# Slot 2's product, GpSimd's slot 1 and the third experts' product in another order, and the tail's input and output on two engines

## The reference

```python
x = x + conv(_gn(x), ...)                   # group norm, a graph convolution, residual
t = _to_tokens(x)
t = t + attn(_ln_t(t), ...)                 # a scan over 1024 tokens, 128 channels x 16 states
t = t + ffn(_ln_t(t), ...)                  # 8 experts, the two best of each token
x = _from_tokens(t, x)

def scan_step(h, inputs):                   # inside attn
    x_t, dt_t, B_t, C_t = inputs
    h_new = exp(dt_t[..., None] * A) * h + (dt_t[..., None] * B_t[:, None, :]) * x_t[..., None]
    return h_new, (h_new * C_t[:, None, :]).sum(axis=-1)

probs = softmax(xt @ Wr + br)               # inside ffn
top_p, top_idx = top_k(probs, 2)
weights = top_p / top_p.sum(axis=-1, keepdims=True)
out = (weights[:, :, None] * take(experts(layernorm(xt)), top_idx)).sum(axis=1)
```

## Time and profile before

| | us |
|---|---|
| median of 3 runs | 381.32 |
| runs | 381.15 to 382.72 |
| profiled execution, its own time | 379.5 |
| its span, first to last instruction | 377.8 |
| VectorE busy | 316.5 (84%) |
| TensorE busy | 317.3 (84%) |
| ScalarE busy | 277.9 (74%) |
| GpSimd busy | 268.0 (71%) |

### The profile page before, as it was taken

The page is one execution under the profiler, slowest core; times in us unless marked ns, Lnnn a source line. Parts: engine busy times, 40 slices in busy tenths (PEclk is TensorE's granted clock), DMA queues, the critical chain, the costliest instruction groups (busy, mean ns, idle before and its releaser), DMA issues. The chain is left out here.

```text
span 377.8 us, 5525 instructions
## 1 busy us (share of the span) xinstructions
PE 317.3 (84%) x1675; PEld 176.7 (47%) x1675; DVE 316.5 (84%) x424; ACT 277.9 (74%) x465; POOL 268.0 (71%) x268
## 2 busy tenths in 40 slices
PE   0597899695899889988998899989987997798795
PEld 0476455441555355525553455345534543453563
DVE  2784457998799989998999899989999998999533
ACT  1002458586989998989899989998988894872483
POOL 8903505685688978897799779977998787877110
PEclk9996999577899999999999999999998999999999
DMA  7934039979989989996996699769957985000000
GB/s 182 250 88 86 2 106 220 228 170 218 222 205 225 225 203 208 220 221 161 219 231 159 152 220 219 152 173 217 222 128 193 224 197 125 3 0 1 16 0 16
DMA packets 21301, 59.54 MB, mean 158 GB/s; under 512 B 4988, under 2 KB 13336, under 8 KB 15384
## 3 DMA queue, kind: packets, MB, share of 16 engines
q1 hardware_dynamic: 20104, 58.35, 68.1%
q10 hardware_dynamic: 1168, 0.84, 0.9%
HBM read 53.94 MB, written 5.24 MB: 157 GB/s over the span
## 5 line engine op out<-in xcount | busy, mean ns | idle before, releaser
L356 POOL TENSOR_TENSOR hs<-hs,Cs 128x1024 f32<-128x1024 f32 x63 | 149.3, 2376 | 22.5 <-DVE hs L836 21.8
L836 DVE TENSOR_TENSOR_SCAN hs<-av,P 128x1024 f32<-128x1024 f32 x64 | 146.3, 2286 | 2.6 <-POOL av L349 0.4
L830 DVE TENSOR_TENSOR P<-P,ub 128x1024 f32<-128x1024 f32 x62 | 76.0, 1226 | 3.1 <-DMA ub<-u_scratch 1.9
L676 ACT ACTIVATE hb<-P,b1c 128x512 f32<-128x512 f32 x112 | 70.1, 685 | 2.4 <-PE P L1309 1.0
L1321 PE MATMUL P<-hb,W2s 128*64 128x256 f32 x448 | 60.3, 392 | 0.0
L1308 PE MATMUL P<-X,W1H 128*128 128x512 f32 x112 | 49.6, 443 | 4.3 <-ACT hb L676 3.3
L617 ACT ACTIVATE av<-P,Aneg 128x510 f32<-128x510 f32 x68 | 44.1, 680 | 9.3 <-PE P L1241 5.2
L1309 PE MATMUL P<-X,W1L 128*128 128x512 f32 x112 | 44.5, 398 | 0.0
L1321 PEld LDWEIGHTS P<-hb,W2s 128*64 128x64 f32 x448 | 27.4, 136 | 27.8 <-issue 17.3
L617 ACT ACTIVATE av<-av,Aneg 128x510 f32<-128x510 f32 x60 | 38.3, 708 | 2.6 <-DMA av<-dt_scratch 2.5
L1241 PE MATMUL P<-D,selD 128*128 128x512 f32 x64 | 29.9, 509 | 11.7 <-ACT av L617 11.4
(11 more groups left out here) (230 smaller groups left out, 546.3 us busy)
## 6 DMA issues: line engine op xcount, KB each, us to landing
ub<-u_scratch SPq DMA_DIRECT2D x31, 1024.0 KB, 11.5
av<-dt_scratch SPq DMA_DIRECT2D x15, 1024.0 KB, 7.3
dt_scratch<-dts SPq DMA_DIRECT2D x7, 256.0 KB, 2.9
u_scratch<-rl SPq DMA_DIRECT2D x7, 256.0 KB, 2.9
av<-in_L_conv_Wr SPq DMA_DIRECT2D x2, 576.0 KB, 6.9
av<-in_L_conv_Wl SPq DMA_DIRECT2D x2, 576.0 KB, 8.6
res<-in_x SPq DMA_DIRECT2D x4, 256.0 KB, 4.5
hb<-in_L_ffn_W SPq DMA_DIRECT2D x2, 512.0 KB, 5.9
```

The source lines that it names most:

```text
L356: gp.tensor_tensor(hs[:, at, :, :], hs[:, at, :, :], rep(Cs[:, p, :], 1, 2), ALU.mult).then_inc(S["cm"], 1)
L676: a_.activation(hb[:, r % HB, :], P[:, F1_BANK[r], :], ACT.Gelu, bias=b1c[:, r:r + 1]).then_inc(S["gl"], 1)
L830: v.tensor_tensor(ring, rep(P[:, BB, :], 1, 2), ub[:, 2 * n:2 * n + 2, :], ALU.mult).then_inc(S["bm"], 1)
L836: v.tensor_tensor_scan(hs[:, (SLOTS * g + n) % RING].rearrange("p a t -> p (a t)"), av[:, 2 * n:2 * n + 2, :].rearrange("p a t -> p (a t)" ...
```

## The change

Four things are written in another order or on another engine; nothing that is computed changes.

- On VectorE the function of a slot is cut into its product and its scan. The product of slot 2 stands ahead of the marks, its scan behind them. The product of slot 7 stands ahead of experts(4), its scan behind.
- On GpSimd slot 1 stands between the split and the weights. It waits for the split's own signal first.
- In the tail VectorE scales xn first, then one half of X2; GpSimd copies the other half from xn. The two differences wait for both.
- The second piece of the last group's result is sent by ScalarE's queue instead of SP's.

```diff
-            sp_out(sp_, G - 1, 1)
+            sp_out(sp_, G - 1, 1, (0,))
...
                     pool_x2(eng, prev)
-                    pool_router(eng, prev)
+                    eng.wait_ge(S["xl2"], prev + 1)
                 if i > 0:
                     pool_slot(eng, i, p, 1)
+                if prev is not None:
+                    pool_router(eng, prev)
...
+            eng.wait_ge(S["xn2"], 2 * G)
+            eng.wait_ge(S["f1"], LAST)
+            gp.tensor_copy(X2[0:64, 0:HW], xn[0:64, :]).then_inc(S["xh2"], 1)
             pool_router(eng, G - 1)
...
+            sp_out(eng, G - 1, 1, (1,))
...
                     dve_router1(eng, prev)
+                dve_product(eng, i, 2)
+                if prev is not None:
                     dve_router2(eng, prev, nxt2)
-                dve_slot(eng, i, 2)
+                dve_scan(eng, i, 2)
...
                 dve_slot(eng, i, 6)
+                dve_product(eng, i, 7)
                 experts(4)
-                dve_slot(eng, i, 7)
+                dve_scan(eng, i, 7)
...
-            for h in range(2):
-                q = slice(64 * h, 64 * h + 64)
-                v.tensor_tensor(X2[q, HW * h:HW * h + HW], P[q, XB, 0:HW], rqs[q, :], ALU.mult).then_inc(S["xh2"], 1)
             v.tensor_tensor(xn, P[:, XB, 0:HW], rqs[:, :], ALU.mult).then_inc(S["xn2"], 2)
+            v.tensor_tensor(X2[64:128, HW:T], P[64:128, XB, 0:HW], rqs[64:128, :], ALU.mult).then_inc(S["xh2"], 1)
             eng.wait_ge(S["xn2"], 2 * G)
-            eng.wait_ge(S["xh2"], 2 * G)
-            for h in range(2):
+            for h in (1, 0):
                 q, o = slice(64 * h, 64 * h + 64), slice(64 - 64 * h, 128 - 64 * h)
+                eng.wait_ge(S["xh2"], 2 * G)
```

More of the change, by code:

```diff
@@ L274, in sp_spread, with sp_out @@
                 sp_.dma_start(ub[:, 4 * c:4 * c + 4, :], rep(u_dram[p][:, 4 * c:4 * c + 4, :], 0, ST)).then_inc(S[f"u_in{c}"], 16)
-        def sp_out(sp_, g, p):
+        def sp_out(sp_, g, p, halves=(0, 1)):
             sp_.wait_ge(S["acc"], EXP * (g + 1))
-            for h in range(2):
+            for h in halves:
                 sp_.dma_start(ov[h, :, g:g + 1, :], acc[64 * h:64 * h + 64, 0:1, :]).then_inc(S["out_sem"], 16)
@@ L817, in dve_slot, with dve_product @@
         def dve_slot(eng, g, n):
+            dve_product(eng, g, n)
+            dve_scan(eng, g, n)
+        def dve_product(eng, g, n):
             c = n // 2
@@ L830, in dve_slot, with dve_scan @@
                 v.tensor_tensor(ring, rep(P[:, BB, :], 1, 2), ub[:, 2 * n:2 * n + 2, :], ALU.mult).then_inc(S["bm"], 1)
+        def dve_scan(eng, g, n):
+            c = n // 2
             eng.wait_ge(S["bm"], SLOTS * g + n + 1)
```

## The result

The changed kernel takes **388.41 us** (median; 386.27 to 391.04) against 382.02 (381.15 to 385.41): a ratio of 1.0168, 95% interval 1.0121 to 1.0214. It is slower, as forecast, but by 6.4 us and not by 3.4, and lies above the range. Its profiled execution took 386.95 us with a span of 385.2, against 379.5 and 377.8. The changed kernel's four executions differ in their mean granted clock, from 0.947 in the fastest to 0.925 in the slowest.

A forecast was written before the change was run, and what follows sets the result against it. Bound by a circle of GpSimd's long run and VectorE's scans 2 to 5. Steps lose 4.23 us, the end gains 0.38 and 0.45: 3.40 lost, 384.7 us, range 380.5 to 386.8.

The forecast's parts named there:

- L902 is held to the slot's end: VectorE's TENSOR_SCALAR in the marks waits until GpSimd's slot 1 ends; scan 2 comes 0.44 us later per step; chance 0.64.
- Slot's end to scan 2, 0.50 us: On VectorE, scan 2 follows the end of GpSimd's slot 1 by 0.50 us, as the product did in step 6.
- The sum of the steps, 4.23 us: Loss over steps 1 to 7: 2.20 us in steps 1 to 5, 0.92 in step 6, 1.11 in step 7.
- Third experts' product behind slot 7's, nothing: On VectorE, slot 7's product ahead of the third experts' product saves waits off the circle; costed at nothing.
- the first rival: L902 isn't held by GpSimd's slot: a step shrinks by about 0.42 us, 3.28 in all, 378.0 us; chance 0.16.
- The weights behind the slot: GpSimd's weights end near 217.9, before TensorE transposes them at 218.38, behind expert products that hide the delay.
- The tail's input and output, -0.38 and -0.45 us: In the tail, sharing the input with GpSimd gains 0.38 us; ScalarE issuing the second last transfer gains 0.45.
- the last rival: L902 held, and TensorE's clock falls before the tail: 0.88 us plus some 1.2 more, 386.8 us; chance 0.10.

The follow-up runs named there:

- The run with two halves: Changed kernel with GpSimd's slot 1 cut into two ops of 128x512 each, all orders kept: 381.89 us, ratio 0.9988 to before.

## Why the prediction was right about the steps and wrong about the tail

*L902 is held to the slot's end*: right. 0.08 us from split to slot was 0.08; 1.6 us of hold was 1.9, as L917 asked 0.49 us into the slot and not 0.77; the end, which alone counts, was the slot's end and 0.02 us. The Trainium skill (SBUF — State Buffer, "Who interferes with whom") says the same: who starts first keeps the shared ports for the whole instruction. The run with two halves agrees, with 0.76 us for the instruction, which ends 0.03 behind the first half. The Trainium skill (VectorE: DVE Perf Modes, "Why PSUM operands drop a tier") says that an operand in PSUM keeps an instruction out of the mode that takes both ports; the run with the result in PSUM agrees, 0.15 us beside a slot. Which mode an instruction ran in, no row shows.

*Slot's end to scan 2, 0.50 us*: it was 0.56, nearly the whole difference between the forecast 0.44 us a step and the 0.51 measured.

*The sum of the steps, 4.23 us*: 4.30. Step 6 gave 1.27, of which 0.39 came back ahead of scan 5 (forecast 1.21 and 0.29), step 7 gave 1.14 (forecast 1.11).

*Third experts' product behind slot 7's, nothing*: right by itself (382.30 us), and the steps of this kernel add up with it at nothing, though no run takes it out of this kernel alone. Wrong for the case without the hold, where it lets slot 2's gain through. So the first rival was mispriced. A step without the hold gains 0.62 us instead of the 0.42 I allowed. As I read it, I took TensorE's waits as the limit and did not see that the third experts' product, and not slot 7's scan, is what has to wait for TensorE. The trace of the kernel with PSUM shows 3.63 us gained from scan 1 of step 1 to the last scan and 0.68 behind it, 4.3 us in all against the 3.28 of the rival. The ratio of the times says 5.9 us, while the two profiled executions stand only 3.3 apart, since this one took 1.0 us longer up to scan 1 of step 1. Where the rest lies, no trace shows.

*The weights behind the slot*: hidden as costed; VectorE's list of waits shows none on TensorE's expert products in the steps.

*The tail's input and output, -0.38 and -0.45 us*: with the clock up, -0.32 and -0.41.

**The step that failed** is the last rival, held at 0.10 and priced at 2.1 us: the sum put TensorE's clock in the tail at nothing. I let "warm-up matmuls stand ahead of the sum" speak against it and put no number to the stop behind them. By my own 1.1 us it would have been 1.62 + 1.1 = 2.7 us, and the sum of the earlier trace rows that ran at 0.50 stands behind a stop of 2.54 us in the trace of before:

```profile
90.43 1.94 PE L1146 MATMUL P<-hs,selS 128*32 128x512 f32 x8 [2.54 <-POOL hs L356]
```

The stop became 2.25 us: the last scan came 4.75 us later than before, the end of the warm-up matmuls only 4.10. The clock fell; with four more of these matmuls the stop was 1.34 us and the clock stayed. The price was short as well. I counted the sum (0.88; measured 0.81) and four short groups (1.2); the chain up to the norm statistics lost 2.03 (4.34 to 6.37) and the router and input 0.53 (2.89 to 3.42), 3.4 us together with the sum. Add it to the forecast of the profiled execution and the rest is the preamble: 382.9 + 3.4 + 0.45 = 386.75, against 386.95.

## What to carry to other kernels

Before a gap on the busiest engine is filled by shifting another engine's long op, look at what will then run at the same moment: here one SBUF-to-SBUF TENSOR_SCALAR of four numbers in each partition stood still for almost 2 us, and writing its result to PSUM turned the loss into a gain of 5.9 us (by the ratio). Price edits in pairs where one only opens the next wait: two moves, neither of which alone could be told from nothing, were worth 4 us together. And when a step shifts an engine that TensorE waits for at a tail, work out the new length of TensorE's stop and what the tail costs at half its clock.

## What the runs showed of the hardware that I had not expected

- The length of the stop ahead of the last sum does not by itself tell in these traces whether TensorE's clock falls. It stood at 1.00 behind 1.62 us (before) and 1.34 (eight warm-ups), and fell to 0.50 during the sum behind 1.70 (two halves), 2.25 and 2.74. With slot 7's product alone (1.34) and the end's edits alone (1.43) the sum still ran at 1.00 in 1.07 and 1.06 us, and the output product behind it, after a second stop of 0.81 us, took 1.12 and 1.05 instead of 0.65. Before had that second stop of 0.81 us too.
- The clock also falls inside the steps, and not in the same place in every execution: in step 7 as told above, and in step 1. With the end's edits alone it was at 0.50 from 95 to 107 us, where before was at 1.00 from 97 on, and scan 2 of step 1 stood 10.94 us behind scan 1 instead of 8.62.
- The first scan came at 56.7 to 59.3 us in the profiled executions of kernels whose work up to there is the same. A difference of 1 us between two of these kernels' times says little unless the trace puts it in a place.
